# Transformer block on one core: each half batch stored by one transfer of 512 KB instead of two of 256 KB, with new instruction orders

## The reference

```python
x = L0_attn_t                                  # (16, 1024, 256)
qkv = einsum('bnd,ed->bne', layernorm(x), W_qkv) + b_qkv
attn = softmax(einsum('bqd,bkd->bqk', Q, K) / sqrt(256))
x = x + layernorm(einsum('bqk,bkv->bqv', attn, V))
z = layernorm(x)
h = silu(z @ w_gate.T / 127) * (z @ w_up.T / 127)   # hidden size 768
x = x + layernorm(h @ w_down.T / 127)
```

## Time and profile before

| | |
|---|---|
| median of 3 runs | 1322.65 us (1322.42 to 1323.86) |
| the profiled execution | 1322.73 us |
| its span, first to last instruction | 1320.9 us |
| TensorE | 1308.1 us busy, 7204 matmuls |
| ScalarE, GpSimd, VectorE | 1019.5, 997.6 and 953.1 us busy |
| DMA queue 1 (SyncE) | 169.67 MB, 65.1% of the 16 engines' span |
| granted TensorE clock | 1.00 of full speed |

### The profile page before, as it was taken

One profiled execution on the slowest core, in us unless ns is written; L12 is line 12 of the kernel. 1 busy time (PEld: TensorE's weight loads), 2 busy tenths in 40 slices (PEclk: granted clock), 3 DMA queues, 4 the chain that ended last, 5 costly groups with the idle time before them and its releaser, 6 DMA issues.

```text
span 1320.9 us, 23123 instructions
## 1 busy us (share of the span) xinstructions
PE 1308.1 (99%) x7204; PEld 705.6 (53%) x7204; DVE 953.1 (72%) x2670; ACT 1019.5 (77%) x1610; POOL 997.6 (76%) x1081
## 2 busy tenths in 40 slices
PE   8999999999999999999999999999999999999998
PEld 5455455555555555455554555545555555555655
DVE  7877686776867768687686867767687686766566
ACT  6768787788878788787887877878777887867655
POOL 4887687786868868687786877878778686875645
PEclk9999999999999999999999999999999999999999
DMA  6887657676656865578666776666767666666422
GB/s 203 158 172 143 147 93 145 130 153 116 120 124 134 167 119 112 122 138 161 125 115 124 130 148 128 142 124 111 144 128 158 116 119 121 136 132 130 92 64 65
DMA packets 492110, 171.96 MB, mean 130 GB/s; under 512 B 473041, under 2 KB 475473, under 8 KB 491986
## 3 DMA queue, kind: packets, MB, share of 16 engines
q1 hardware_dynamic: 491184, 169.67, 65.1%
q10 hardware_dynamic: 802, 0.79, 0.2%
HBM read 36.70 MB, written 16.78 MB: 40 GB/s over the span
## 4 chain that ended last, share of the span: by engine, by line
PE 90%; POOL 3%; issue 2%; ACT 2%; DMA 2%; SPq 1%; DVE 1%; POOLq 0%; ACTq 0%; DVEq 0%
PE S L1073 71%; PE S L1232 17%; POOL Pl L449 1%; DMA yTl<-yl 1%; SPq L309 1%; DMA PTh<-Ph 1%; POOL qTl L426 0%; POOL yl L476 0%; PE S L1102 0%; PE S L1155 0%; ACT xh L558 0%; SPq L278 0%; ACT P L614 0%; SPq L321 0%; POOL xl L401 0%
## 5 line engine op out<-in xcount | busy, mean ns | idle before, releaser
L449 POOL TENSOR_TENSOR Pl<-P,Ph 128x1024 f16<-128x1024 f32 x128 | 271.4, 2131 | 52.4 <-issue 37.8
L1073 PE MATMUL S<-PTh,xh 128*128 128x512 f16 x512 | 194.1, 379 | 0.0
L1073 PE MATMUL S<-PTl,xh 128*128 128x512 f16 x512 | 194.0, 379 | 0.0
L1073 PE MATMUL S<-PTh,xl 128*128 128x512 f16 x512 | 194.0, 379 | 0.0
L651 ACT ACTIVATE hf<-S,sc 128x512 f32<-128x512 f32 x192 | 129.3, 684 | 64.8 <-PE S L1073 52.8
L614 ACT ACTIVATE P<-P,nmx,sc 128x1024 f32<-128x1024 f32 x112 | 138.2, 1234 | 43.4 <-DVE nmx L901 43.2
L1073 PE MATMUL S<-Wh,hTh 128*128 128x256 f16 x768 | 170.2, 273 | 0.4 <-DVE X L986 0.4
L1073 PE MATMUL S<-Wh,hTl 128*128 128x256 f16 x768 | 170.2, 273 | 0.0
L364 POOL TENSOR_TENSOR rs<-rs,mhalf 128x4 f32<-128x4 f32 (+2 forms) x160 | 146.0, 912 | 13.3
L485 POOL TENSOR_TENSOR hTl<-hf,hTh 128x512 f16<-128x512 f32 x128 | 146.8, 1157 | 8.6 <-ACT hTh L658 5.6
L895 DVE CUSTOM_DVE_ANT_0 P<-S,P 128x512 f32<-128x512 f32 x112 | 76.9, 689 | 96.7 <-ACT P L581 46.6
(11 more groups left out here) (206 smaller groups left out, 3295.6 us busy)
## 6 DMA issues: line engine op xcount, KB each, us to landing
xs<-in_L_attn_t SPq DMA_DIRECT2D x32, 512.0 KB, 4.6
X<-in_L_attn_t SPq DMA_DIRECT2D x32, 512.0 KB, 4.6
out_x<-X SPq DMA_DIRECT2D x62, 256.0 KB, 2.9
PTh<-Ph SPq DMA_TRANSPOSE x128, 3.7
PTl<-Pl SPq DMA_TRANSPOSE x128, 3.3
hTh<-in_L_ffn_w_up SPq DMA_DIRECT2D x1, 768.0 KB, 6.9
hTl<-in_L_ffn_w_down SPq DMA_DIRECT2D x1, 768.0 KB, 8.4
hTl<-in_L_ffn_w_gate SPq DMA_DIRECT2D x1, 768.0 KB, 9.8
```

The costliest lines, as they stand in the source:

```text
L449: p.engine.tensor_tensor(out=Pl[:, m % 3, :], in0=P[:, m % 4, :], in1=Ph[:, m % 3, :], op=ALU.subtract).then_inc(pl_vector if i in PL_ON_V ...
L1073: done = t.engine.matmul(out, s, m, start=(start and i == 0), stop=(stop and i == len(terms) - 1))
```

## The change

Each half batch is stored by one transfer that waits for both pairs, and `stored` counts 16 for a half batch in place of 32. All five engines' lists are made anew (with the moments at which transfers land drawn at random while they are made); the instructions in them are the same but for the stores. The core of the diff:

```diff
         def reload(s, b, g):
             n = 2 * b + g
             k = n % 3
-            s.wait_ge(stored[k], 32 * (n // 3))
+            s.wait_ge(stored[k], 16 * (n // 3))
...
-        def store(s, b, g, pair):
-            k, pr = (2 * b + g) % 3, slice(2 * pair, 2 * pair + 2)
-            s.wait_ge(fin_done[pair], 2 * b + g + 1)
-            s.engine.dma_start(
-                out_d[b, :, :].rearrange("(p t) d -> p t d", t=NT)[:, 4 * g + 2 * pair:4 * g + 2 * pair + 2, :], X[k][:, pr, :]
-            ).then_inc(stored[k], 16)
+        def store(s, b, g):
+            k = (2 * b + g) % 3
+            s.wait_ge(fin_done[0], 2 * b + g + 1)
+            s.wait_ge(fin_done[1], 2 * b + g + 1)
+            s.engine.dma_start(out_d[b, :, :].rearrange("(p t) d -> p t d", t=NT)[:, 4 * g:4 * g + 4, :], X[k][:, :, :]
+                               ).then_inc(stored[k], 16)
```

SyncE, the start and the loop:

```diff
             load_x(s, 0, 0)
             load_x(s, 0, 1)
-            load_x(s, 1, 0)
             load_ffn(s, 1)
             load_ffn(s, 2)
+            load_ffn(s, 0)
+            load_x(s, 1, 0)
             load_x(s, 1, 1)
-            load_ffn(s, 0)
+            load_x(s, 2, 0)
             turn_x(s, 1, 0, 0)
-            load_x(s, 2, 0)
...
                 turn_p(s, b + 1, 1, 0)
                 turn_x(s, b + 2, 0, 0)
                 turn_x(s, b + 2, 0, 1)
-                turn_p(s, b + 1, 2, 0)
                 turn_y(s, b, 0, 0)
                 turn_y(s, b, 0, 1)
...
-                turn_p(s, b + 1, 7, 0)
+                turn_p(s, b + 2, 0, 0)
+                reload(s, b + 1, 0)
                 turn_p(s, b + 2, 0, 1)
-                store(s, b, 0, 0)
-                store(s, b, 0, 1)
+                store(s, b, 0)
+                reload(s, b + 1, 1)
                 turn_p(s, b + 2, 1, 1)
-                turn_p(s, b + 2, 0, 0)
-                reload(s, b + 1, 1)
```

ScalarE's loop, the places that the prediction speaks of:

```diff
+                add_bias(a, b, 0, 0)
+                exp(a, b + 2, 2)
                 x_hat(a, b + 3, 0)
-                x_hat(a, b + 3, 1)
+                x_high(a, b + 3, 0)
                 copy_m1(a, b + 2, 2)
-                x_high(a, b + 3, 0)
-                exp(a, b + 2, 2)
-                add_bias(a, b, 0, 0)
+                exp(a, b + 2, 3)
                 copy_u2(a, b + 2, 2)
                 p_high(a, b + 2, 2)
+                p_high(a, b + 2, 3)
+                copy_u3(a, b + 2, 2)
                 o_high(a, b + 1, 1, 1)
-                copy_u3(a, b + 2, 2)
-                exp(a, b + 2, 3)
-                p_high(a, b + 2, 3)
-                o_high(a, b + 1, 1, 0)
                 y_hat(a, b + 1, 0, 0)
                 y_hat(a, b + 1, 0, 1)
+                o_high(a, b + 1, 1, 0)
                 y_high(a, b + 1, 0)
```

VectorE's and GpSimd's loops, and TensorE's:

```diff
-                d_add(v, b, 0, 0)
-                sum_11(v, b + 2, 0)
                 x_stats(v, b + 3, 0)
-                d_add(v, b, 0, 1)
                 sum_21(v, b + 2, 0)
                 sum_22(v, b + 2, 0)
+                sum_11(v, b + 2, 0)
                 sum_12(v, b + 2, 0)
+                d_add(v, b, 0, 1)
                 sum_11(v, b + 2, 1)
+                o_low(v, b + 1, 0, 1)
+                row_inverse(v, b + 1, 1)
                 x_stats(v, b + 3, 1)
-                o_low(v, b + 1, 0, 1)
                 sum_21(v, b + 2, 1)
+                d_add(v, b, 0, 0)
                 sum_22(v, b + 2, 1)
                 o_low(v, b + 1, 0, 0)
...
                 h_low(p, b, 1, 1)
-                d_norm(p, b, 0, 0)
+                h_low(p, b, 1, 3)
                 p_low(p, b + 1, 5)
                 p_low(p, b + 1, 6)
+                p_low(p, b + 1, 7)
+                x_norm(p, b + 3, 0)
+                h_low(p, b, 1, 4)
+                d_norm(p, b, 0, 0)
                 d_norm(p, b, 0, 1)
...
                 attend_part(t, b + 1, 0, 4, (hmul_done, 12 * b + 11))
+                attend_part(t, b + 1, 0, 5)
                 pair_first(t, b + 2, 0, (silu_done, 12 * b + 9), (hl_vector, 4 * b + 3), (silu_done, 12 * b + 12), (hl_vector, 4 * b + 4))
-                attend_part(t, b + 1, 0, 5)
```

SyncE's end:

```diff
-            store(s, 14, 1, 0)
-            store(s, 14, 1, 1)
-            store(s, 15, 0, 0)
-            store(s, 15, 0, 1)
+            store(s, 15, 0)
+            store(s, 14, 1)
             store_last(s, 0)
             store_last(s, 1)
```

More of the change, by code:

```diff
@@ L1382, in _ @@
-            turn_ffn(s, 0, 0)
             turn_p(s, 0, 7, 0)
-            turn_p(s, 0, 6, 0)
             turn_p(s, 0, 7, 1)
             turn_ffn(s, 0, 1)
+            turn_p(s, 0, 6, 1)
+            turn_ffn(s, 2, 0)
             reload(s, 0, 0)
+            reload(s, 0, 1)
             turn_p(s, 1, 0, 1)
[L1389 to L1392, removed]
+            turn_ffn(s, 1, 0)
+            turn_p(s, 1, 1, 1)
@@ L1393, in _ @@
             turn_ffn(s, 1, 1)
             turn_x(s, 2, 0, 1)
-            turn_x(s, 2, 1, 0)
[L1396 to L1402, removed]
+            turn_p(s, 1, 0, 0)
+            turn_p(s, 1, 1, 0)
+            turn_ffn(s, 2, 1)
+            turn_y(s, 0, 0, 0)
+            turn_y(s, 0, 0, 1)
+            load_x(s, 3, 0)
@@ L1403, in _ @@
+            turn_t(s, 2, 0, 0)
+            turn_x(s, 2, 1, 0)
             turn_x(s, 2, 1, 1)
-            turn_p(s, 1, 1, 1)
-            turn_p(s, 1, 3, 0)
             turn_y(s, 0, 1, 0)
             turn_y(s, 0, 1, 1)
-            load_x(s, 3, 0)
-            turn_t(s, 2, 0, 0)
+            turn_p(s, 1, 2, 0)
+            turn_p(s, 1, 3, 0)
+            turn_t(s, 2, 0, 1)
+            turn_p(s, 1, 3, 1)
+            turn_p(s, 1, 2, 1)
+            turn_p(s, 1, 5, 0)
+            turn_t(s, 2, 1, 0)
@@ L1410, in _ @@
+            turn_t(s, 2, 1, 1)
+            load_x(s, 3, 1)
+            turn_p(s, 1, 4, 0)
+            turn_p(s, 1, 4, 1)
+            turn_p(s, 1, 6, 1)
+            turn_p(s, 1, 5, 1)
+            turn_p(s, 1, 7, 1)
+            turn_p(s, 1, 7, 0)
             reload(s, 1, 0)
             turn_p(s, 1, 6, 0)
[L1412 to L1423, removed]
             turn_p(s, 2, 0, 1)
-            store(s, 0, 0, 1)
+            store(s, 0, 0)
             reload(s, 1, 1)
@@ L1576, in _ @@
             h_low(p, 0, 0, 3)
+            q_low(p, 2, 0)
             h_low(p, 0, 0, 4)
-            p_low(p, 1, 4)
-            q_low(p, 2, 0)
-            x_norm(p, 3, 0)
+            d_norm(p, 0, 0, 0)
             h_low(p, 0, 1, 0)
             h_low(p, 0, 1, 1)
-            d_norm(p, 0, 0, 0)
             t_low(p, 2, 1)
+            p_low(p, 1, 4)
+            x_norm(p, 3, 0)
             p_low(p, 1, 5)
             p_low(p, 1, 6)
+            h_low(p, 0, 1, 3)
+            h_low(p, 0, 1, 4)
+            p_low(p, 1, 7)
+            x_norm(p, 3, 1)
+            x_low(p, 3, 0)
             d_norm(p, 0, 0, 1)
-            x_low(p, 3, 0)
-            p_low(p, 1, 7)
             p_low(p, 2, 0)
             q_low(p, 2, 1)
-            h_low(p, 0, 1, 3)
-            x_norm(p, 3, 1)
             p_low(p, 2, 1)
@@ L1598, in _ @@
             p_low(p, 2, 3)
-            h_low(p, 0, 1, 4)
             y_low(p, 1, 0)
@@ L1658, in _ @@
             p_low(p, 14, 6)
-            h_low(p, 13, 1, 4)
+            d_norm(p, 13, 0, 1)
+            q_low(p, 15, 1)
             p_low(p, 14, 7)
@@ L1668, in _ @@
             p_low(p, 15, 3)
+            h_low(p, 13, 1, 4)
+            y_norm(p, 14, 1)
             p_low(p, 15, 4)
-            y_norm(p, 14, 1)
+            p_low(p, 15, 5)
+            x1_norm(p, 14, 1)
             d_norm(p, 13, 1, 0)
-            x1_norm(p, 14, 1)
             h_low(p, 14, 0, 0)
@@ L1694, in _ @@
             h_low(p, 15, 0, 0)
+            d_norm(p, 14, 1, 1)
             h_low(p, 15, 0, 1)
-            d_norm(p, 14, 1, 1)
             h_low(p, 15, 0, 3)
+            h_low(p, 15, 0, 4)
             d_norm(p, 14, 1, 0)
-            h_low(p, 15, 0, 4)
+            d_norm(p, 15, 0, 1)
             h_low(p, 15, 1, 0)
-            d_norm(p, 15, 0, 1)
             h_low(p, 15, 1, 1)
@@ L1833, in _ @@
             x_hat(a, 3, 1)
-            exp(a, 2, 3)
-            o_high(a, 1, 1, 1)
+            p_high(a, 2, 2)
             copy_u3(a, 2, 2)
-            p_high(a, 2, 2)
             p_high(a, 2, 3)
             y_hat(a, 1, 0, 0)
+            o_high(a, 1, 1, 1)
+            exp(a, 2, 4)
+            o_high(a, 1, 1, 0)
             y_hat(a, 1, 0, 1)
-            o_high(a, 1, 1, 0)
+            copy_m1(a, 2, 3)
             y_high(a, 1, 0)
-            exp(a, 2, 4)
-            copy_m1(a, 2, 3)
             p_high(a, 2, 4)
@@ L1990, in _ @@
             y_high(a, 14, 0)
+            o_high(a, 14, 1, 0)
             o_high(a, 14, 1, 1)
@@ L2193, in _ @@
             x1_add(v, 1, 0, 1)
-            o_low(v, 1, 1, 1)
+            sum_21(v, 2, 2)
+            sum_11(v, 2, 2)
             row_inverse(v, 2, 0)
-            sum_11(v, 2, 2)
-            sum_21(v, 2, 2)
             sum_22(v, 2, 2)
@@ L2200, in _ @@
             o_low(v, 1, 1, 0)
+            o_low(v, 1, 1, 1)
             sum_11(v, 2, 3)
```

(7 more changed lines are left out.)

500 lines of the change are left out of this document (245 added, 255 removed).

## The result

The changed kernel took 1325.43 us (median of 16 runs, 1324.93 to 1325.90), the kernel before 1322.41 us beside it (16 runs, 1321.73 to 1323.86). The ratio is 1.0023, 95% interval 1.0016 to 1.0030. The forecast was 1322.0 us and no measurable change; the time lies 0.07 us inside the upper edge of the range, 1325.5, which had been set by a rival that did not occur, and on the side to which I had given 0.20.

The account below looks back on a forecast made before the run. TensorE was taken as the bound, busy 1308.1 of 1320.9 us. From the profiled 1322.73 us, 0.6 for yTl was subtracted and 0 added for the rest: 1322.1, or 1322.0 against the median; 8-in-10 range 1320.4 to 1325.5.

Parts of the forecast that it names:

- (1) The stores: Loop, SyncE: merged 512 KB store issued near 633.5 instead of 639.80 us, landing in 4.6; new reload wait costs TensorE nothing.
- (2) The tight edge: Loop: ScalarE's 1.79 us wait goes, yTl's transpose is issued almost 2 us sooner, TensorE's yTl wait goes; gain 0.6 us.
- (3): TensorE's instruction order: parts of attention exchange places with score products, the same matmuls; 0 us.
- (4) The project_v edge: Loop, o_low before project_v: moved d_add shrinks the room from 0.42 to about 0.25 us; cost 0, bound 0.3 us a batch.
- The slower rival, a wait in every pass: Loop, project_v waits on a late o_low: 0.5 us late gives 3.3 us, 1325.3; 0.8 late gives 1329; chance 0.19.
- (5) The head: Kernel start: three FFN weight loads issued earlier might delay W_qkv's landing at 7.8 us; cost 0, bound some 5.5 us.
- the third rival's: Kernel start: FFN loads share DMA with W_qkv, up to 2.8 us later less 1.0 room: 1.8 us, 1323.8; chance 0.09.
- what was issued earlier went first: Kernel start: reading of the old trace's DMA queues 1 and 10, used to price W_qkv's delay from the FFN loads at 0.
- (6) The tail: Kernel end: store(15, 0) ahead of store(14, 1), both out near 1312 and done about 1316.3 us; cost 0, bound 1 us.
- The sum: Whole kernel: 1322.73 us profiled, less 0.6 for yTl, plus 0 for the rest; forecast 1322.0 against the median.

## Why the prediction was wrong, step by step

**(1) The stores: right.** In the loop of the changed kernel (TensorE's work in this pass stands 1.6 us later than before):

```profile
635.31 0.62 SPq L322 DMA_DIRECT2D out_x<-X  x1
639.12 0.33 SPq L298 DMA_DIRECT2D X<-in_L_attn_t  x1
639.50 1.24 SPq L309 DMA_TRANSPOSE PTl<-Pl  x1
```

The store goes at 635.31 instead of 639.80, the reload stands behind it until it has landed, and `turn_p(b + 2, 1, 1)` goes at 639.50. I had 633.5, 638 and 638.5, to which the shift of the pass is to be added. With the 1.6 us added, the three are right within half a microsecond. The new wait is there, and no wait of TensorE belongs to it. SyncE's waits, whole span:

```profile
SPq L36 <- ACT X L666: 121.0, 15, 20.7
...
SPq L298 <- DMA out_x<-X: 57.7, 15, 5.2
```

The median over all stores is 3.4 us, but it mixes two kinds: in the loop those of (b, 1) land in 2.9 to 3.4 us, and those of (b, 0), which the reload waits for, in 3.8 to 5.8 us (3.8 in the lines above, 57.7 / 15 = 3.85 us of waiting in the mean). For these the 4.6 that I took was of the right size.

**(2) The tight edge: right, and worth more.** `y_hat` starts when its input from GpSimd is there, and yTl's transpose is issued at 653.07 against 653.75 although the pass is 1.6 us later, so 2.3 us sooner, where almost 2 was forecast:

```profile
647.33 2.08 ACT L634 ACTIVATE yn<-X,nb,rs 128x256 f32<-128x256 f32 x4 [1.56 <-POOL nb L369]
...
653.07 1.23 SPq L315 DMA_TRANSPOSE yTl<-yl  x1
```

The gain is 1.1 us, not 0.6: the list of waits had two stalls with 0.6 us, the spacing of matmuls has three with 1.2 us (at 495, 657 and 1141 us).

**(3) "TensorE's own order ... the same matmuls; 0 us": this step failed**, and first. The 0.85 us at 146.75 us come from exactly such an exchange. I had read a twin of it at 1218 us in the earlier trace rows, named its cause (a round trip between `pair_second` and `pair_third`), and checked only whether that one would stay, not whether the diff made another; in the head the diff moves `attend_part(1, 1, 4)` out from between. The step asked only whether the matmuls are the same, and the sum has no term at all for the moved calls of VectorE, ScalarE and GpSimd in the head. The experiments add that it is not repaired in one place. Put back, the wait returns at the next edge (1.23 us), and with that repaired too, at the next (0.85 us). Nor is it TensorE's list alone: with only that one old, nothing comes back. What costs is the new head as a whole: with the old one 2.3 us come back. Which of its calls make up the loss beyond the gap at 147 us stays open.

**(4) The project_v edge: cost right, room not.** `d_add` and `o_low` of the changed kernel, and the matmul that waits for them:

```profile
631.12 0.87 DVE L1034 SCALAR_TENSOR_TENSOR X<-S,rs,X 128x256 f32<-128x256 f32 x2
...
632.82 0.68 DVE L952 SCALAR_TENSOR_TENSOR oTl<-S,oTh 128x512 f16<-128x512 f32 x1
634.10 0.27 PE L1073 MATMUL S<-Vh,oTh 128*128 128x256 f16 x1
```

The room is 634.10 - 633.50 = 0.60 us; I had 0.25, so it grew from 0.42 where I had it shrink. (The threshold that I gave for this rival was a little low: 0.2% above the kernel before needs 2.65 + 0.6 = 3.25 us, 0.25 in each of 13 passes, so 0.50 us of lateness, not 0.47.) The slower rival, a wait in every pass, did not occur, although the time came out where it would have: right size, other mechanism.

**(5) The head: the mechanism was the third rival's, its price less.** Queues 1 (SyncE) and 10 (ScalarE) of the changed kernel, in the windows from 2.5, 6.5 and 7.5 us, each 1 us long (packets, MB, share):

```profile
q1 hardware_dynamic: 67, 0.27, 98.5%
...
q10 hardware_dynamic: 203, 0.20, 56.5%
q1 hardware_dynamic: 181, 0.19, 52.0%
...
q1 hardware_dynamic: 188, 0.19, 55.8%
q10 hardware_dynamic: 188, 0.18, 53.7%
```

From 2.5 to 3.5 us queue 10 got nothing, as before; but once the FFN loads were at the front of queue 1, both queues moved the same 0.19 MB in the same microsecond. The Trainium skill ("DMA: Bandwidth & Descriptors", Queues, rings and completion order) has each DMA engine take turns between queue rows packet by packet. What the profile counts as a packet need not be what the page means, but with packets of some 1 KB on both sides, 203 of queue 10 and 181 of queue 1, the trace agrees with equal turns. The two transfers of `W_qkv` landed after 7.7 and 8.8 us:

```profile
hTh<-in_L_attn_W_qkv ACTq DMA_DIRECT2D x1, 512.0 KB, 7.7
hTh<-in_L_attn_W_qkv ACTq DMA_DIRECT2D x1, 256.0 KB, 8.8
```

and TensorE, which could start sooner because the bias came 0.7 us earlier, waited 0.86 us:

```profile
9.00 1.99 PE L1117 MATMUL S<-hTh 128*128 128x256 f32 x8 [0.86 <-DMA hTh<-in_L_attn_W_qkv]
...
17.90 0.38 PE L1189 MATMUL S<-xTh,zTh 128*128 128x512 f16 x1 [0.71 <-ACT zTh L570]
```

The second half landed some 2 us late, near the 1.8 to 2.8 us of that rival, but 9.00 is only 0.18 us behind 8.82, and at the first score matmul 0.30 us are left. Two experiments with the loads early in an old head show no cost that can be measured. I had given this mechanism 0.09 on a remark that the old trace shows no sharing. That was misread, from two windows between which the sharing lay. From 4.5 to 5.5 us of the trace of before:

```profile
q1 hardware_dynamic: 84, 0.29, 72.6%
q10 hardware_dynamic: 89, 0.09, 28.7%
```

The packets are about equal in number, and the bytes three to one, because those of x are the larger ones: that fits turns by packet, not by byte, and not "what was issued earlier went first". Why queue 10 moved nothing between 2.5 and 3.5 us stays open.

**(6) The tail: "Cost 0; bound 1 us": this step failed too.** It cost 1.0 + 0.56 us, more than the bound. I priced only the stores, not the moved calls of the other engines. Of the 1.0 us of new stalls, 0.33 stand before `project_v(15, 1)` and 0.32 before `down(15, 0, 1)`, which is now ahead of `gate_up(15, 1, 2)` and must wait for X (L1034). The old end takes them away, and 0.9 us of the median. The stores themselves:

```profile
1314.30 1.55 SPq L322 DMA_DIRECT2D out_x<-X  x2
1318.49 2.47 SPq L328 DMA_DIRECT2D out_x<-X  x2
```

Issues and time to landing:

```profile
out_x<-X SPq DMA_DIRECT2D x2, 512.0 KB, 5.4
out_x<-X SPq DMA_DIRECT2D x1, 384.0 KB, 3.8
out_x<-X SPq DMA_DIRECT2D x1, 128.0 KB, 2.6
```

With a start at 1314.30 and 5.4 us for each, not the 3.2 that I took for 1 MB, they are still landing when the next store is issued. From the last sum into X to the end: 2.83 to 2.92 us in the seven kernels with the old end (the one before among them), 2.90 to 3.65 us in the ten with the new end (the changed kernel 3.48). The difference lies in the landing of the very last store, of 128 KB: it is issued 0.5 us behind the last sum in all 17 kernels and lands in 1.9 us in the seven, in 1.9 to 2.7 in the ten. In two of the ten the two 512 KB stores had landed 0.3 us or more before the last sum, and there the last store takes 1.9 us; in seven they land 0.1 to 0.9 us behind it, and it takes 2.1 to 2.7. The tenth, with the two stores exchanged, does not fit (landed 0.3 us before, and still 2.3). So the late landing of the big stores goes with the longer end, but that it is the cause is not shown.

Also open is the stall of 0.35 us at 1063.5 us for X (L986), one pass of twelve: it is there, 0.40 to 0.41 us, in the nine kernels in which VectorE, ScalarE and GpSimd follow the new head, and in none of the five with the new loop in which they follow the old, 900 us behind it. The 0.2 us at 209 us go with the same nine. What carries the difference that far was not looked for.

**The sum.** Foreseen -0.6; measured -1.1 (yTl), +0.3 (start, within the spread of executions, see the last section), +1.2 and +0.2 (head), +0.35 (1063 us), +1.0 (tail), +0.56 (last landing) = +2.5 of 2.7 us in the profiled pair.

## What to carry to other kernels

When a kernel's bound engine is 99% busy and all lists are remade, price the part outside the loop call by call: the loop repeats and was probably balanced, while each new neighbour in head and tail can open a round trip of its own. For every stall known in the old trace, write down the pair of calls that makes it and search the whole diff for a new pair of the same kind. Then treat the engines' lists as one thing: here SyncE's list and the other four taken from different heads cost 11 and 16 us against the changed kernel, and the version with the lowest median took whole stages, not single repairs, from either kernel.

## What the runs showed of the hardware

- Two queues shared the DMA engines nearly evenly by the profile's count of packets: 181 and 203 packets of some 1 KB in one microsecond (0.19 and 0.20 MB), and, where queue 1 had the larger packets of x, 84 and 89 packets (0.29 and 0.09 MB). From 2.5 to 3.5 us, with 67 packets of 4 KB on queue 1, queue 10 moved nothing.
- A 512 KB store to memory landed in 3.4 us (median of the changed kernel; 2.6 to 5.8 us for single ones), a 512 KB load of x in 4.2 us by the same page; two such stores issued together in 5.4 us.
- When TensorE had stood idle for 4.1 us, the granted clock was 0.50, its lower level of 1.2 GHz, for the following 5 us, in which 512-column matmuls started every 0.43 us instead of 0.216. The spacings over the regular one add up to 2.8 us behind that wait of 4.1 us.
- Short waits can have such a stretch behind them too. In the head of two profiled executions the clock was 0.50 for 3.4 us: from 9.2 us behind a wait of 1.86 us for `W_qkv`, and from 13.1 us where no wait since 7.7 us had been longer than 0.52 us, which made the first score matmul 1.5 us later. The waits of up to 0.9 us in the profiled executions of the kernels before and after had none, nor had one of 1.9 us at 152 us in the run with SyncE's old head.
- Leaving out those two executions, the first score matmul started between 17.37 and 18.03 us in four kernels with the same old head, and between 17.63 and 18.02 us in five with the new one. One execution's head is not to be read finer than that; the +0.30 us of the table is within this spread.
